# Blocked inverses with a turned transpose, split exponentials, and bf16 terms subtracted in PSUM

## Time and profile before

| what | value |
|---|---|
| time, median of 3 runs | 1788.99 us (1785.4 to 1790.18) |
| the profiled execution | 1789.75 us, its span 1788.0 us |
| busy over the span | PE 1250.5 us (70%), DVE 1332.3 (75%), ACT 879.0 (49%), POOL 248.0 (14%) |
| granted clock of PE | 0.801 on average |

### The profile page before, as it was taken

How to read it: one execution, slowest core, us unless ns; L and a number is a source line. 1 busy time by engine, 2 the same in 40 slices (tenths; PEclk the granted TensorE clock), 3 DMA queues, 4 the chain that set the end, 5 groups by cost and what they waited for, 6 DMA issues and landing times. The chain is left out here.

```text
span 1788.0 us, 29542 instructions
## 1 busy us (share of the span) xinstructions
PE 1250.5 (70%) x10539; PEld 612.1 (34%) x10540; DVE 1332.3 (75%) x3509; ACT 879.0 (49%) x1678; POOL 248.0 (14%) x274
## 2 busy tenths in 40 slices
PE   4799999999999997566973543040314789833776
PEld 2122222222222224346962431020113456622445
DVE  5899999999999953365448236959697779667773
ACT  4079999999999996221211113040002446612453
POOL 4000000000000000013310333030003231100223
PEclk9589999999999999667995676575655797965668
DMA  1101100001000000000004431000001402021000
GB/s 56 49 2 28 28 21 20 20 26 30 22 20 20 20 2 16 1 28 1 1 1 181 112 77 33 0 1 1 0 0 38 140 11 52 21 103 56 21 22 30
DMA packets 43229, 58.57 MB, mean 33 GB/s; under 512 B 11993, under 2 KB 33564, under 8 KB 42684
## 3 DMA queue, kind: packets, MB, share of 16 engines
q1 hardware_dynamic: 37851, 49.95, 9.4%
q0 software_dynamic: 3968, 6.01, 1.3%
q10 hardware_dynamic: 1264, 0.72, 0.2%
HBM read 29.81 MB, written 13.63 MB: 24 GB/s over the span
## 5 line engine op out<-in xcount | busy, mean ns | idle before, releaser
L724 ACT ACTIVATE l0att_probs<-l0att_ps_sv 128x512 f32<-128x512 f32 x1024 | 555.9, 595 | 84.4 <-PE l0att_ps_sv L694 72.6
L761 DVE TENSOR_REDUCE l0att_half_negmax<-l0att_ps_m 128x1 f32<-128x1024 f32 x480 | 547.2, 1215 | 6.3 <-PE l0att_ps_m L633 6.3
L663 PE MATMUL l0att_ps_sv<-l0att_probs,l_V_aug 128*32 128x256 f32 x4096 | 331.2, 392 | 5.3 <-ACT l0att_pv_sb L715 5.3
L694 PE MATMUL l0att_ps_sv<-l_Q,l_K 51*128 51x512 bf16 x1024 | 201.0, 389 | 2.5 <-ACT l0att_probs L724 0.2
L633 PE MATMUL l0att_ps_m<-l_K,l_Q 48*128 48x512 bf16 x960 | 186.1, 385 | 11.1 <-DVE l0att_half_negmax L761 7.1
L663 PEld LDWEIGHTS l0att_ps_sv<-l0att_probs,l_V_aug 128*32 128x32 f32 x4096 | 83.3, 108 | 199.1 <-issue 104.7
L694 PEld LDWEIGHTS l0att_ps_sv<-l_Q,l_K 51*128 51x128 bf16 x1024 | 49.6, 93 | 216.7 <-ACT l0att_probs L724 204.1
L350 PE MATMUL ada_ps<-ident_sb,xn 128*128 128x128 f32 x112 | 31.3, 442 | 87.5 <-DVE xn L338 87.0
L413 POOL CAST l0att_nm<-l0att_negmax 128x16 bf16<-128x16 f32 x16 | 3.2, 198 | 514.1 <-DVE l0att_negmax L737 514.1
L2554 ACT ACTIVATE l3loc_probs<-l3loc_ps_s 128x320 f32<-128x320 f32 x128 | 48.9, 435 | 36.1 <-PE l3loc_ps_s L2533 35.5
L2030 PE MATMUL l2spk_ps<-l_X,l_spikes_l_w2T 128*128 128x512 f32 x32 | 16.5, 680 | 68.3 <-DVE l_X L2054 68.3
(11 more groups left out here) (598 smaller groups left out, 2355.9 us busy)
## 6 DMA issues: line engine op xcount, KB each, us to landing
l_Q<-l_qp SPq DMA_DIRECT2D x188, 32.0 KB
l_K<-l_kp SPq DMA_DIRECT2D x188, 32.0 KB
l1ffn_W<-in_l_expert_w_dram SPq DMA_DIRECT2D x1, 4096.0 KB
l3f_experts_l_w<-in_l_w_dram SPq DMA_DIRECT2D x2, 2048.0 KB
l_sorted_in<-l1ffn_zeros SPq DMA_DIRECT2D x1, 3072.0 KB
l1exp_rows<-l_sorted_in SPq DMA_DIRECT2D x6, 512.0 KB, 8.5
l_sorted_out<-l1exp_y SPq DMA_DIRECT2D x6, 512.0 KB
l_Q<-l_q_parts SPq DMA_DIRECT2D x18, 128.0 KB
```

What stands on the lines that cost most here:

```text
L663: mm = pe.matmul(ps_v[32 * c:32 * c + 32, cols], V_aug[:, kt, h, :], probs[:, kt % 2, c, cols], start=(kt == 0 and part == 0), stop=(kt == ...
L694: pe.matmul(ps_s[:, (n + i) % 3, :], K[at, h % HEAD_BUFS, c1(kt)], Q[at, h % HEAD_BUFS, c4(2 * pair + i)], start=True, stop=True).then_inc ...
L724: act.activation(probs[:, kt % 2, c, :], ps_s[:, n % 3, :], ACT.Exp).then_inc(expd, 1)
L761: dve.tensor_reduce(half_negmax[:, h % 2, t, half:half + 1], src, AX_X, ALU.max, negate=True).then_inc(m_read, 1)
```

## The change

- **Projections.** k comes first, then q. The weights of q are scaled once by ACT, in place of a scale in every copy. ACT copies a bank's high term; PE then adds minus that term to the same bank (a bf16 matmul with -I, `minus16`, a new constant), DVE copies what is left as the middle term, PE subtracts this too, and the rest is copied as the low term, by DVE for even banks and by ACT for odd ones. PE's list runs two and four banks behind the full products. V is copied a bank at a time. POOL's and DVE's subtractions and the float32 copy of k go; q's stays in layer 3.
- **Inverses.** `join` makes only T; X is T turned by four transposes on PE (`turn`) and copied by ACT. The last level computes only the upper right 64x64 corner of X: `reach` and `join_corner` on 64 columns, and DVE writes minus the result into X.
- **Latent.** DVE takes minus the maxima; four of the eight heads are exponentiated one by one straight from PSUM, with the maximum as bias and the sum taken in the same instruction (`accum_out`); DVE subtracts and sums only the other four. A score bank is free once its exponentials are done, not once the subtraction is.
- **Mask rows.** POOL loads them for all heads of `Q[0]`, `K[0]`, `Q[1]`, `K[1]` from DRAM by four DMAs, in the projection's block behind two memsets; DVE's copies go. SP stores k's terms before q's, each as soon as it is there. ACT's copies for `Q[2]`, `K[2]` stay.

```diff
@@ -421,82 +421,104 @@
+        def term(n, i):
+            return (kp, qp)[n // NC4][i][:, c4(n % NC4)]
+
...
             @block.tensor
             def _(pe):
                 pe.wait_ge(loads.done, loads.all)
+                for s in range(CHUNKS + 4):
+                    if s < CHUNKS:
+                        if s == NC4:
+                            pe.wait_ge(scaled, 1)
+                        pe.matmul(ps[:, s, :], w[:, 1 - s // NC4, :], g.hT[:, c4(s % NC4)], start=True, stop=True,
+                                  skip_group_check=True).then_inc(full_done, 1)
+                    if 2 <= s < CHUNKS + 2:
+                        n = s - 2
+                        pe.wait_ge(high_read, n + 1)
+                        pe.matmul(ps[:, n, :], minus[:], term(n, 0), start=False, stop=True,
+                                  skip_group_check=True).then_inc(rest_done, 1)
+                    if s >= 4:
+                        n = s - 4
+                        pe.wait_ge(middle_read, n + 1)
+                        pe.matmul(ps[:, n, :], minus[:], term(n, 1), start=False, stop=True,
+                                  skip_group_check=True).then_inc(last_done, 1)
+                    if s >= CHUNKS:
+                        j = s - CHUNKS
+                        pe.wait_ge(low_read[j % 2], j // 2 + 1)
+                        for t in range(4 * j, 4 * j + 4):
+                            mm = pe.matmul(ps[:, j, c1(t % 4)], g.hT[:, c1(t)], w[:, 2, :], start=True, stop=True)
                         mm.then_inc(v_done, 1)
...
             @block.scalar
             def _(act):
+                act.wait_ge(loads.done, loads.all)
+                act.activation(w[:, 0, :], w[:, 0, :], ACT.Identity, scale=L0_K ** -0.5).then_inc(scaled, 1)
+                for s in range(CHUNKS + 4):
+                    if s < CHUNKS:
+                        act.wait_ge(full_done, s + 1)
+                        if q is not None and s >= NC4:
+                            act.activation(q[:, c4(s - NC4)], ps[:, s, :], ACT.Identity)
+                        act.activation(term(s, 0), ps[:, s, :], ACT.Identity).then_inc(high_read, 1)
+                    n = s - 4
+                    if n >= 0 and n % 2 == 1:
+                        act.wait_ge(last_done, n + 1)
+                        act.activation(term(n, 2), ps[:, n, :], ACT.Identity).then_inc(low_read[1], 1)
+                    j = s - CHUNKS
+                    if j >= 0:
+                        act.wait_ge(v_done, j + 1)
+                        act.activation(V_aug[:, 4 * j:4 * j + 4, :, 0:L0_K],
+                                       ps[:, j, :].rearrange("p (t h k) -> p t h k", t=4, h=L0_H), ACT.Identity)
...
-                    dve.wait_ge(parts_done, n + 1)
+                for s in range(CHUNKS + 2):
+                    if s < CHUNKS:
+                        dve.wait_ge(rest_done, s + 1)
+                        dve.tensor_copy(term(s, 1), ps[:, s, :]).then_inc(middle_read, 1)
+                    n = s - 2
+                    if n >= 0 and n % 2 == 0:
+                        dve.wait_ge(last_done, n + 1)
+                        dve.tensor_copy(term(n, 2), ps[:, n, :]).then_inc(low_read[0], 1)
...
-                pool.wait_ge(pool_parts_done, 1)
+                if beside is not None:
+                    beside(pool)
                 pool.wait_ge(v_filled, 2)
@@ -1264,45 +1285,67 @@
...
+                def reach(n):
+                    l, j = n // NC4, n % NC4
+                    if j == 0:
+                        pe.wait_ge(c_ready, l + 2)
+                    if n == 0:
+                        pe.wait_ge(x_copied, NC4)
+                        pe.wait_ge(m_copied, NC4)
+                    pe.wait_ge(x_copied, n + 1)
+                    if n >= 2:
+                        pe.wait_ge(y_copied, n - 1)
+                    for t in range(4):
+                        i = 4 * j + t
+                        if n < JOINS:
+                            mm = pe.matmul(ps_y[:, n % 2, c1(t)], C[:, (l + 1) % 2, i, :], X[:, i, :], start=True,
+                                           stop=True)
                         else:
+                            mm = pe.matmul(ps_y[0:HALF, n % 2, corner(t)], C[HALF:P, (l + 1) % 2, i, 0:HALF],
+                                           X[HALF:P, i, HALF:P], start=True, stop=True)
+                    mm.then_inc(y_done, 1)
+
+                def join(n):
+                    pe.wait_ge(y_copied, n + 1)
+                    if n >= 2:
+                        pe.wait_ge(t_ready, n - 1)
+                    for t in range(4):
+                        mm = pe.matmul(ps_t[:, n % 2, c1(t)], Y[:, n % 2, c1(t)], T[:, 4 * (n % NC4) + t, :], start=True,
+                                       stop=True)
+                    mm.then_inc(t_done, 1)
+
+                def turn(n):
+                    pe.wait_ge(t_ready, n + 1)
+                    if n >= 2:
+                        pe.wait_ge(x_copied, NC4 + n - 1)
+                    for t in range(4):
+                        mm = pe.transpose(ps_x[:, n % 2, c1(t)], T[:, 4 * (n % NC4) + t, :], g.ident[:])
+                    mm.then_inc(x_turned, 1)
+
+                def join_corner(j):
+                    pe.wait_ge(y_copied, JOINS + j + 1)
+                    pe.wait_ge(t_ready, min(JOINS + j - 1, JOINS))
+                    if j >= 2:
+                        pe.wait_ge(corner_ready, j - 1)
+                    for t in range(4):
+                        mm = pe.matmul(ps_t[0:HALF, j % 2, corner(t)], T[0:HALF, 4 * j + t, 0:HALF],
+                                       Y[0:HALF, j % 2, corner(t)], start=True, stop=True)
+                    mm.then_inc(corner_done, 1)
+
+                for n in range(JOINS + NC4 + 1):
+                    if n < JOINS + NC4:
+                        reach(n)
+                    if 1 <= n <= JOINS:
+                        join(n - 1)
+                    if n > JOINS:
+                        join_corner(n - JOINS - 1)
+                    if 2 <= n < JOINS + 2:
+                        turn(n - 2)
                 for j in range(NC4):
                     if j == 0:
...
@@ -1329,11 +1372,21 @@
...
+                for n in range(JOINS + NC4):
                     act.wait_ge(y_done, n + 1)
                     if n >= 2:
-                        act.wait_ge(tx_done, n - 1)
-                    act.activation(Y[:, n % 2, :], ps_y[:, n % 2, :], ACT.Identity).then_inc(y_copied, 1)
+                        act.wait_ge(t_done, min(n - 1, JOINS))
+                    if n < JOINS:
+                        act.activation(Y[:, n % 2, :], ps_y[:, n % 2, :], ACT.Identity).then_inc(y_copied, 1)
+                    else:
+                        if n >= JOINS + 2:
+                            act.wait_ge(corner_done, n - JOINS - 1)
+                        act.activation(Y[0:HALF, n % 2, 0:4 * HALF], ps_y[0:HALF, n % 2, 0:4 * HALF],
+                                       ACT.Identity).then_inc(y_copied, 1)
+                    if 2 <= n < JOINS + 2:
+                        act.wait_ge(x_turned, NC4 + n - 1)
+                        act.activation(tiles(X, (n - 2) % NC4), ps_x[:, n % 2, :], ACT.Identity).then_inc(x_copied, 1)
                 for j in range(NC4):
@@ -1355,13 +1408,14 @@
...
+                for n in range(JOINS):
+                    dve.wait_ge(t_done, n + 1)
+                    dve.tensor_tensor(tiles(T, n % NC4), tiles(T, n % NC4), ps_t[:, n % 2, :], ALU.subtract)\
+                       .then_inc(t_ready, 1)
+                for j in range(NC4):
+                    dve.wait_ge(corner_done, j + 1)
+                    dve.tensor_scalar(X[0:HALF, 4 * j:4 * j + 4, HALF:P], ps_t[0:HALF, j % 2, 0:4 * HALF].rearrange(
+                        "p (t f) -> p t f", t=4), -1.0, None, ALU.mult).then_inc(corner_ready, 1)
@@ -2170,18 +2224,11 @@
 
...
-
-
-def copy_mask_rows(copy, operand, buf, copied):
@@ -2271,7 +2321,7 @@
...
                     else:
-                        pe.wait_ge(sub_ready, t - 3)
+                        pe.wait_ge(expd, t - 3)
@@ -2328,7 +2378,13 @@
...
-                        act.activation(probs[:, t % PROBS], sc[:, t % 2], ACT.Exp).then_inc(expd, 1)
+                        if t >= 2:
+                            act.wait_ge(rden_ready, t - 1)
+                        for h in range(SUMMED):
+                            act.activation(probs[:, t % PROBS, h, :],
+                                           ps_a[:, t % 4, h * LATENTS:(h + 1) * LATENTS], ACT.Exp,
+                                           bias=neg_top[:, t % 2, h:h + 1], accum_out=den[:, t % 2, h:h + 1])
+                        act.activation(probs[:, t % PROBS, SUMMED:], sc[:, t % 2], ACT.Exp).then_inc(expd, 1)
@@ -2359,22 +2415,22 @@
...
                                       ALU.mult).then_inc(gkv_ready, 1)
-                for operand in (Q, K):
...
```

(21 more changed lines are left out.)

## The result

The changed kernel takes 1766.89 us (median of 4 runs, 1764.48 to 1767.36), beside it the kernel before 1789.08: ratio 0.9875, interval 0.9861 to 0.9889. It is 22 us faster, where 22.1 were forecast. The total came out, two of its parts did not: the projections gave twice what I had for them, and layer 1's state stage, which the change does not touch, took 8.7 us back in the profiled execution. That these two came out nearly even is luck.

A forecast was written before the change was run, and what follows sets the result against it. No engine fills the span: PE alone bounds layer 1's inverses, DVE's subtractions the projections' end, a ring of engines the latent loop. Terms 12.6 + 4.2 + 1.3 + 4.0 = 22.1 us give 1767 us, range 1760 to 1778.

The forecast's parts named there:

- Inverses, 12.6: Layer 1's inverses: transposes for join X in 20 steps save 8.9 us, the last level's corners 3.7.
- The last level: End of layer 1's inverses: work on 64 columns takes 4.6 us for 8.3, 3.7 less (bounds 0.2 to 4.0).
- My 1.0: Last level of the inverses: copies, reach, corner and negation add about 1.0 us to eight steps of 3.6.
- Projections, 4.2: Projections of layers 0 and 3: PE's bf16 subtractions save 2.2 us in layer 0 and 2.0 in layer 3.
- my upper bound of 2.9: Projections of layers 0 and 3: most each could gain, in us; layer 0's path 17.1 for 20.0 at 0.22 a matmul.
- Latent head, 1.3: Start of the latent stage: shorter PE idling may keep the clock, loop up to 2.7 us earlier or nothing; 1.3 taken.
- Loop, 4.0: Latent loop: DVE's subtraction and sum on 256 columns for 512 save 0.27 us a tile, 4.3 for 16; 4.0 taken.
- Masks by POOL, nothing: Mask rows by POOL's DMAs: loaded by about 1450 us, read from 1471.50 on, so they cost nothing.
- a rival: Inverses: transposes drop PE's clock to 0.50, 20 steps cost 44 us more than forecast, corner 4: 1815 us; chance 0.04.
- as dear as a join: Rival in the inverses: a turn costs what a join did, 8.9 us lost, 1776 us; chance 0.08.
- ACT did not bound the loop: Rival in the latent loop: ACT becomes its bound through the sums, 1772 to 1775 us; chance 0.10.
- the projections gained more, not nothing: Rival: projections gain nothing as engines hand banks to and fro, 4.2 and 1.3 us lost, 1773 us; chance 0.08.

The follow-up runs named there:

- both runs on heads: Changed kernel with none, then two, of the heads exponentiated one by one in place of four: 1768.92 us (ratio 0.9887) and 1767.75 us (0.9880).
- the extra matmuls: Changed kernel with two extra float32 matmuls of 128 columns in every chunk of the state stage, into an unread PSUM bank: 1764.73 us, ratio 0.9877.

## Why the prediction was right, and where it was not

- **Inverses, 12.6: measured 12.8** (12.9 and 12.6 in the two pairs). The step is 2.22 as forecast, a transpose one record of 0.11; undone alone the turns cost 9.2 to 9.5 for 8.9. The last level gives 3.15 for 3.7, as the run with full tiles has it: in place of 8.3 it takes 5.1 for my 4.6. My 1.0 for what its chain adds to the eight steps should have been 1.5.
- **Projections, 4.2: measured 8.9.** This is the term that I had wrong. Layer 0 gave 4.1 for 2.2, layer 3 4.8 for 2.0. I took a value between 0.22 and 0.31 for the bf16 matmul; it was 0.22, the lower end, so both ought to have stood at my upper bound of 2.9. Layer 3's rows end 2.9 earlier (19.67 to 16.7). The other 1.8 there are the term I left out: behind the last part the kernel before issued three stores on SP, 1.62 us, before the next stage could begin; the change issues all but one of them earlier. That this made the 1.8 is read from the trace, it was not tried alone. I had told of those stores only as traffic. In layer 0 the rows end 3.2 earlier (20.0 to 16.8 with a late rise of the clock), the hand-over to the loads is 0.3 shorter, and 0.5 lies behind the first load, of unknown cause.
- **Latent head, 1.3: 0.9** (first matmul to first maximum 13.0, now 12.1). I had two cases, the clock lasts over the gap (2.7) or not (nothing), and took the middle. It lasted, and the first eight records gained the 2.7; then it fell, and the records behind them lost 1.8.
- **Loop, 4.0: 3.2** (first maximum to last 48.0, now 44.8). The steady period is right; I multiplied the gain of the steady part by all 16 tiles, but there are 15 gaps, and the first ones wait for other things. An exponential of 64 columns with its sum starts 0.29 after the one before, for my 0.25 without.
- **Masks by POOL, nothing: nothing.** The local attention starts 1.0 us behind the latent stage, for 1.0 to 1.1 before.
- **Not in the sum: the clock behind the inverses.** Terms of 12.8, 8.9, 0.9 and 3.2 make 25.8. In the first pair of profiles 8.7 went back in the state stage and 5 came by other moments of the clock and by the last row, mostly in the rows of layers 0 and 1, which makes the 22.4 between the two spans; in the second pair 0.9 went back there and 2 in other rows: 23.1. So the total was right because a gain too small by 4 met a loss that I had priced only as a rival: I had PE's clock fall in the inverses, where it held at 1.00. It fell behind them.

What the runs show on that loss: in all seven profiles with transposes in the inverses and W and U in a block behind them, the granted clock fell for a while, at some time from 880 to 898 us, in the products for W and U or early in the state stage (twice the changed kernel, full tiles, both runs on heads, the old projections, the extra matmuls). In the seven others (twice the kernel before, old inverses, turns by a matmul, three with W and U between the corners) it did not. The state stage was 27.9 to 28.1 us where the clock was full in it, and 28.7, 33.1 and three times 36.5 where it was not. Corners aren't needed for it, and the shift in time alone doesn't do it. Why W and U between the corners avoid it with as many transposes was not settled, so the cause of the fall stays open.

The Trainium skill, "TensorE: Matmul & The Clock Gate", section "Part 4: PE-mode transpose", says that transposes don't count as work for the clock gate. I had set it aside on the ground of the loop's 1.00. Turned into matmuls, the same tiles kept the clock in the one profile of that run, so the runs lean to the rule; a fifth of PE's time in transposes at 1.00 for 30 us shows that it takes more than their presence.

Undone one at a time, against a mean ratio of 0.987 for the change, the inverses are worth 0.55 points, the projections 0.59, the heads 0.17 (9.8, 10.5 and 3.0 us, each uncertain by 3 or more). Together they are 23.3, and the whole change is 23; with such uncertainties this says only that no large part is missing. The inverses' share in runs is lower than in their own stage, 9.8 for 12.8; what the clock takes back would explain it, but the difference is no larger than the uncertainty.

The rivals: the clock did not fall in the inverses; a turn was not as dear as a join; ACT did not bound the loop; the projections gained more, not nothing.

## What to carry to other kernels

A stage that gets shorter changes what PE does just ahead of the next one; where that next stage is a chain of small matmuls that needs the full clock, price a clock lost there as a term of the sum and not only as a rival. When a tail is removed, count the DMA issues that stood behind it on their queue. Compare stages over at least two profiled executions of each kernel before a difference is put down to the change: here stages untouched by it differed by 3, and by 8 us where the clock had fallen. Even two that agree can mislead: behind the latent stage both profiles of the changed kernel had 311.0 us, and its variants, with the same code there, from 309.3 to 313.8.

## What was not expected of the hardware

- With the clock at 0.50 the state stage kept PE busy for 23.79 of 24.00 us and the grant did not rise; by the profile's busy time, a busy PE at the low level is not by itself on its way back.
- The moment at which the clock rises in layer 0's projection differs between executions of one kernel (first attention matmul at 42.10 and 45.02, before at 48.17 and 46.22).
- The sum of an exponential is an extra record, ACTIVATION_READ_ACCUMULATOR, of 0.21 us, but it overlaps: four rows of 64 columns with their sums start 0.29 us apart, for 0.25 without sums.
